# A spectral layer on one core: two images half a block apart, one image's transforms between the pieces of the other's MLP

## What is computed

```python
for i in range(L):                       # 4 blocks
    residual = x
    xn = layer_norm(transpose(x))        # over the 64 channels
    xf = rfft2(xn, norm='ortho')         # 128 x 65, complex
    o1 = relu(xf @ w1 + b1)              # complex, 64 -> 64
    o2 = o1 @ w2 + b2                    # complex
    o2 = o2 * ((|o2r| > 0.01) | (|o2i| > 0.01))
    x = residual + irfft2(o2)
    h = gelu(layer_norm(x) @ mw1 + mb1)  # 64 -> 256
    x = x + (h @ mw2 + mb2)              # 256 -> 64
```

## Time and profile before

| | us |
|---|---|
| median of 3 runs | 4481.55 |
| the profiled execution's own time | 4472.71 |
| its span | 4470.9 |
| TensorE busy | 3373.0 (75%) |
| VectorE busy | 2843.4 (64%) |
| ScalarE busy | 2372.6 (53%) |
| GpSimd busy | 1225.0 (27%) |
| ScalarE table loads in the spectral layer | 28 of 1.28 us |

### The profile page before, as it was taken

The page is one execution under the profiler, slowest core; times in us unless marked ns, Lnnn a source line. Parts: engine busy times, 40 slices in busy tenths (PEclk is TensorE's granted clock), DMA queues, the critical chain, the costliest instruction groups (busy, mean ns, idle before and its releaser), DMA issues. The chain is left out here.

```text
span 4470.9 us, 55410 instructions
## 1 busy us (share of the span) xinstructions
PE 3373.0 (75%) x18880; PEld 2122.3 (47%) x18880; DVE 2843.4 (64%) x4911; ACT 2372.6 (53%) x3931; POOL 1225.0 (27%) x869
## 2 busy tenths in 40 slices
PE   4957777787587878788687878785777778777559
PEld 1744444544263636363535353633545454534327
DVE  3866666666566666664766666656666666638748
ACT  2944545454445454545454545454454545446538
POOL 3321414141214141411131323222141414114232
PEclk9978888898798989898898989897888889889869
DMA  9810000000000000010000000001000000044498
GB/s 253 264 61 1 5 1 5 1 4 38 39 4 1 4 1 4 1 42 39 4 1 5 1 5 1 5 38 42 1 5 1 5 1 4 38 173 143 131 257 248
DMA packets 218637, 209.36 MB, mean 47 GB/s; under 512 B 53344, under 2 KB 181472, under 8 KB 209648
## 3 DMA queue, kind: packets, MB, share of 16 engines
q1 hardware_dynamic: 190832, 174.84, 12.3%
q10 hardware_dynamic: 19552, 16.79, 1.6%
q0 software_dynamic: 7968, 13.99, 1.2%
HBM read 125.84 MB, written 79.69 MB: 46 GB/s over the span
## 5 line engine op out<-in xcount | busy, mean ns | idle before, releaser
L1495 ACT ACTIVATE a_hidden<-a_wide,a_up_b 128x1024 f32<-128x1024 f32 x512 | 545.8, 1111 | 160.8 <-PE a_wide L1606 160.8
L1606 PE MATMUL a_wide<-a_yc,a_up_fold 64*128 64x512 f32 x2048 | 557.0, 666 | 68.2 <-ACT a_yc L1478 63.7
L1515 PE MATMUL a_bank<-a_dft_w,a_y 128*128 128x128 f32 x2048 | 265.4, 297 | 383.5 <-issue 178.4
L1350 DVE TENSOR_TENSOR a_x<-a_bank,a_x 128x512 f32<-128x512 f32 x256 | 177.1, 692 | 558.7 <-PE a_bank L1625 553.4
L1616 PE MATMUL a_bank<-a_hidden,a_down 128*64 128x512 f32 x2048 | 496.0, 605 | 0.0
L1232 POOL TENSOR_TENSOR a_y<-a_x,a_stat 128x512 f32<-128x512 f32 x256 | 265.9, 1043 | 717.8 <-PE a_bank L1595 393.6
L1515 PEld LDWEIGHTS a_bank<-a_dft_w,a_y 128*128 128x128 f32 x2048 | 261.0, 212 | 391.0 <-issue 389.0
L1606 PEld LDWEIGHTS a_wide<-a_yc,a_up_fold 64*128 64x128 f32 x2048 | 189.0, 199 | 400.0 <-issue 222.4
L1595 PE MATMUL a_bank<-a_ident,a_y 128*128 128x128 f32 x1024 | 167.2, 289 | 251.8 <-POOL a_y L1232 251.8
L1557 PEld LDWEIGHTS a_wide<-a_mix,a_o 128*128 128x128 f32 x2080 | 273.7, 191 | 129.8 <-issue 122.4
L1371 DVE TENSOR_REDUCE a_stat<-a_sq 128x16 f32<-128x1024 f32 x224 | 271.2, 1211 | 98.9 <-ACT a_sq L1472 98.9
(11 more groups left out here) (220 smaller groups left out, 6852.5 us busy)
## 6 DMA issues: line engine op xcount, KB each, us to landing
a_g<-turned SPq DMA_DIRECT2D x20, 1024.0 KB, 7.7
box_x<-in_x SPq DMA_DIRECT2D x64, 256.0 KB, 4.4
turned<-box_o SPq DMA_DIRECT2D x64, 256.0 KB, 3.8
rows<-a_x SPq DMA_DIRECT2D x16, 1024.0 KB, 6.9
box_x<-rows SPq DMA_DIRECT2D x16, 1024.0 KB, 23.4
...
```

The lines of the kernel that those rows point to most:

```text
L1495: A(hidden[:, q % 2, j], wide[j][:], ACT.Gelu, bias=up_b[:, HC + j:HC + j + 1]).then_inc(s_hid, 1)
L1515: mm = M(bank[i % 4][:, c * P:(c + 1) * P], y[:, 4 * i + c, :], dft_w[:], start=True, stop=True)
L1606: mm = M(wide[j][:, half * BANK:(half + 1) * BANK], up_fold[cs, j * P:(j + 1) * P], yc[cs, q % 2], start=True, stop=True)
```

## The change

The spectral layer becomes one block without barriers or loops, in which all 16 runs are written out. Run n is image `n // 8 * 2 + n % 2` and layer `n // 2 % 4`: two images alternate. A period (n, q) holds MLP block q of run n; the transforms of run n + 1, the other image, are cut into 59 parts and put between its pieces by a table, with four slots in each block. Periods go from n = -2 (statistics of the first image) to the end of run 15.

```diff
-STRIP_ORDER = (0, 1, 7, 2, 6, 3, 5, 4)
+U_INVERSE, U_FORWARD, U_SPECTRUM, U_BACKWARD, U_NEXT, U_END = 0, 4, 20, 39, 55, 59
+def parts_before(slot):
+    if slot <= 18:
+        return sum(slot > s for s in (2, 4, 16, 17))
+    if slot <= 22:
+        return U_FORWARD + 4 * (slot - 18)
+    if slot <= 41:
+        return U_SPECTRUM + slot - 22
+    if slot <= 45:
+        return U_BACKWARD + 4 * (slot - 41)
+    return U_NEXT + sum(slot > s for s in (45, 46, 50, 52))
...
-        low_banks = [psum(f"bank{i}") for i in range(4)]
-        wide = [psum(f"wide{i}", 2 * BANK) for i in range(2)]
+        wide = psum("wide", 2 * BANK)
+        turned, result = psum("turned"), psum("result")
+        bank = [psum(f"bank{i}") for i in range(4)]
...
-        y = sb("y", [P, C, P])
+        y = [sb(f"y{i}", [P, C, P]) for i in range(2)]
-        xf = sb("xf", [P, 2, BANK])
-        o1 = sb("o1", [P, 2, BANK])
-        mag = sb("mag", [P, 2, 4, 2, C])
+        stage = sb("stage", [P, 2, SH, C])
+        xf = sb("xf", [P, BANK])
+        o1 = sb("o1", [P, BANK])
+        mag = sb("mag", [P, 4, 2, C])
...
+                def mlp_up(i, j):
+                    pe.wait_ge(s_yc, i + 1)
+                    if i or j:
+                        pe.wait_ge(s_hid, HC * i + j)
...
                 def mlp_down(i):
                     pe.wait_ge(s_hid, HC * (i + 1))
-                    if q >= 1:
-                        pe.wait_ge(s_delta, q)
+                    if i:
+                        pe.wait_ge(s_res, i)
...
+                for n, q in periods():
+                    Q = BLOCKS * n + q
+                    mlp = 0 <= Q < BLOCKS * RUNS
+                    if mlp:
+                        mlp_up(Q, 0)
+                    parts(n, q, 0, inverse, forward, spectrum, backward)
+                    if 0 <= Q - 2 < BLOCKS * RUNS:
+                        turn_back(Q - 2)
+                    if 0 <= Q + 1 < BLOCKS * RUNS:
+                        turn(Q + 1)
+                    parts(n, q, 1, inverse, forward, spectrum, backward)
+                    if mlp:
+                        mlp_up(Q, 1)
+                    parts(n, q, 2, inverse, forward, spectrum, backward)
+                    if 0 <= Q - 1 < BLOCKS * RUNS:
+                        mlp_down(Q - 1)
+                    parts(n, q, 3, inverse, forward, spectrum, backward)
-            clear(nc, sems)
-            nc.all_engine_barrier()
```

More of the change, by code:

```diff
@@ new lines, in afno_layers @@
+        centre = room[:, 6 * L * P:6 * L * P + P]
+        s_const, s_wscaled, s_wfold, s_wready = (sem(n) for n in ("const", "wscaled", "wfold", "wready"))
+        s_w = [sem(f"w{i}") for i in range(L)]
+        s_raw = [sem(f"raw{i}") for i in range(2)]
+        s_spill, s_reload = [sem(f"spill{i}") for i in range(8)], [sem(f"reload{i}") for i in range(8)]
+        s_stage_out = [sem(f"stage_out{i}") for i in range(2)]
+        s_stage = sem("stage")
+        s_step, s_act_step = sem("step"), sem("act_step")
@@ L1055, in copy_spectrum, with periods, parts @@
             return copy(g[0:HALF + 1, 1:KW - 1, 1, cs], im[0:HALF + 1])
+        def periods():
+            for n in range(-2, RUNS + 1):
+                for q in range(BLOCKS if n < RUNS else 2):
+                    yield n, q
+        def parts(n, q, s, inverse, forward, spectrum, backward):
+            for u in parts_in(q, s):
+                if u < U_FORWARD:
+                    if 0 <= n < RUNS:
+                        inverse(n, INVERSES // 2 + u)
+                elif 0 <= n + 1 < RUNS:
+                    if u < U_SPECTRUM:
+                        forward(n + 1, u - U_FORWARD)
+                    elif u < U_BACKWARD:
+                        spectrum(n + 1, u - U_SPECTRUM)
+                    elif u < U_NEXT:
+                        backward(n + 1, u - U_BACKWARD)
+                    else:
+                        inverse(n + 1, u - U_NEXT)
         with nc.Block() as block:
@@ L1161, in _ @@
+            @block.scalar
+            def _(act):
+                A = nc.scalar.activation
+                count = [0]
+                with nc.allow_non_contiguous_dma("small weights"):
+                    act.dma_start(centre, const[CENTRE]).then_inc(s_const, 16)
+                    for l in range(L):
                         loads = []
@@ L1663, in afno_layers @@
+        clear(nc, sems)
         nc.all_engine_barrier()
```

1129 lines of the change are left out of this document (539 added, 590 removed).

## The result

The changed kernel takes 4517.37 us (median of 5 runs, 4510.91 to 4528.12), the kernel before in the same session 4473.92 (5 runs). The ratio is 1.010, 95% interval 1.0077 to 1.0124: 1% slower, where 4275 us, 4.6% faster, had been forecast. The number lies inside the range, the direction is wrong. The profiled execution has a span of 4513.4 us, against 4470.9.

The account below looks back on a forecast made before the run. TensorE was nearest to a bound inside the stages, idle between them. Runs of 210 us gave 490 + 2940 + 200 + 98 + 30 = 3758; with 504 for box layers, span 4262, forecast 4275 us, range 3960 to 4560.

Parts of the forecast that it names:

- TensorE's work per run: All matmuls of one run at full clock, summed from the old kernel's product times: 162.6 us.
- the clock: TensorE's granted clock halves beside long gaps, five a run: taken as 5 us, between ends of 0 and 13.
- blocks 12 to 3: MLP blocks 12 to 15 and 0 to 3, without transforms, mlp_down waiting for the residual: 63.3 us a run.
- blocks 4 to 11: MLP blocks with the transforms between: 117 us of TensorE work and 21 of waits, 138 us a run.
- the reload: Strip 1's reload waits for GpSimd's next_y and lands 2 to 5 us late: 3 us a run.
- the forecast run of 210: One whole run: 63.3 + 138 + 3 + 5 = 209, taken as 210 us.
- the backward gap: Ahead of the backward transform TensorE waits for masks queued in VectorE with block 9's sums and root: 9.5 us.
- The port: VectorE masks and roots meeting GpSimd's next_y and fold: taken as 0, otherwise 10 us a run, 150 in all.
- The sum by that rule, 4425: Rival: GpSimd's port and late strips hold VectorE, 10 us a run more; chance 0.10 with its upper part to equal.
- Rival 3: Clock stays down in MLP-only blocks, 32 us a run more, 4755 us; 0.18 with any mixture above 4504.
- Rivals 1 and 4: TensorE stays the bound, runs 175 to 190, 3900 us, chance 0.20; table loads, some 80 us a run, under 1%.
- Start and end: Forward transform starts about 356, first MLP block about 490; 30 us for staging copies; box layers 504 behind.

Follow-up runs that it names:

- run 2: Not an experiment: one layer of one image, one of 16 runs inside the changed kernel, profiled in windows: 223.8 us, TensorE busy 183.12 and idle 40.7.
- experiment 7: The split kernel with GpSimd's next_y and fold cut to 4 of 64 channels: 4070.58 us; also ten extra products on the kernel of experiment 6: 4270.16 us.
- the split kernel: The changed kernel with the reduction of squares and the root behind the next residual in blocks 9, 12, 13, 0 and 1: 4237.05 us, ratio 0.9475.
- experiment 4: The changed kernel with ten unused products of 128 columns ahead of mlp_down in blocks 1, 2, 13 and 14: 4464.52 us, ratio 0.9983.
- experiment 1: The changed kernel with VectorE's sums and roots behind the next residual: six MLP-only blocks 4462.8 us, block 9 only 4380.25, all blocks 4370.29.
- experiment 3: The changed kernel with GpSimd's next_y and fold cut to 4 of 64 channels, so another output: 4388.82 us, ratio 0.9817.
- experiment 6: The split kernel with half of the 88 weight loads issued by SyncE instead of ScalarE: 4206.81 us, ratio 0.9403.
- run 14: Not an experiment: the last but one of the 16 runs inside the changed kernel, 197.8 us, forecast as 200 with half the sums.

## Why the forecast was wrong

**The step that failed is TensorE's work per run**, the sum of 162.6 us at full clock with 5 for the clock: 167.6. Run 2 of the changed kernel has 183.12, 15.5 more. The waits were forecast as 38.9 (17.9 in blocks 12 to 3, 21 in blocks 4 to 11) and 3 for the reload, 41.9, and measured as 40.7. So of the 14 us that lie between the forecast run of 210 and the measured 223.8, all lie in the busy time, by these windows.

The trace divides the 15.5. In five stretches of run 2 the granted clock is 0.5 (992.3 to 999.2, 1053.8 to 1057.2, 1125.5 to 1139.1, 1180.1 to 1183.5, 1190.3 to 1197.1). The sum of their windows:

```profile
sum 34.10, PE 22.05 PEld 10.33 DVE 17.40 ACT 5.08 POOL 16.31; mean PE 4.41 PEld 2.07 DVE 3.48 ACT 1.02 POOL 3.26
```

TensorE is busy for 22.05 us of these 34.10. At the higher clock that work would take about half (eight products 1.94 us instead of 3.68), so as an estimate the clock costs 11.0 us where 5 stood, and at full clock the work is 172.1 us where 162.6 stood. **Both terms of the sum were too small, the work by 9.5 us and the clock by 6.0.**

Part of that could have been seen. The windows of the forecast give 2851.99 us of busy time in the layer, 178.2 for each of 16 runs, and 175.24 in run 1. Of these 17.03 fall at the lower clock, by the same count, so the old run needs 166.7 us at full clock, and 4.1 us of the 9.5 are missing from the forecast's reading of the old kernel already. The other 5.4 came with the change, and closing the gaps doesn't remove them. The kernel with the fewest gaps, in experiment 7, has this run:

```profile
899.80:1094.30 194.50, 175.44 (x976) 105.87 (x974) 126.86 (x240) 118.12 (x180) 31.67 (x42) 0.98 0.13 44
```

At a clock of 0.98 TensorE is still busy 175.44 us, 172.7 of them at full clock by the same estimate; the split kernel's run has 172.5. The forecast took distances between starts from the old kernel's longer trains. Cut into pieces, the same products stand further apart at full clock. The two halves of an up product take 1.06 us each to the next start (1171.58 to 1172.63 above), where the old one took 1.92 for both (674.71 to 676.63). A piece of the backward transform takes 3.77 (1141.91 to 1145.68) for 16 products, where the forecast has 3.53. A chunk of the spectrum takes 2.75 (1068.29 to 1071.04) for 2.65, an inverse piece up to 1.91 (1167.80 to 1169.71) for 1.72. With 16 blocks, 8 pieces of the transforms, 16 chunks and 8 inverse pieces that makes about 8 of the 9.5 us. Why a cut costs this was not tested.

By groups, the forward transform's products took 14 us less in all (297 ns before, 282 after), and mlp_down took 76 more, the up product 51 and mix 36. Experiment 4, which raises the clock in the four blocks, gives back 73 of the 76, 26 of the 51 and 3 of the 36: in mlp_down it was the clock, in mix hardly at all.

**Blocks 12 to 3.** Forecast 63.3, with 3 and some of the 5 on top; measured 71.9. The long and the short ones are those forecast: blocks 13, 14, 1 and 2 long, blocks 15, 12, 3 and 0 short, though block 13, without its inverse piece, is as long as block 14 and not shorter. Experiment 1 shows the chain to be the cause, and experiment 4 gives 5.0 of the 8.6 us to the clock. The mechanism was right, its consequence for the clock too small: a wait of 3.95 us is followed by 1.45 us more in the product.

**Blocks 4 to 11.** Forecast 138, measured 152.8. TensorE's work, 117, was 127.56 in run 2. Of the waits, the backward gap was taken as 9.5 and is 13.3 on the mean; the mix products' wait was taken as 2 and is 6.2. In run 2 the waits of these blocks are 24.4 against 21, those of blocks 12 to 3 are 16.3 against 17.9 and 3 for the reload, so the total of 41.9 was met in part by luck. The queue of masks, sums and root was named rightly: moving block 9's sums, in experiment 1, gave 137 us. The 3.8 beyond it are close to the 3.2 that one pair of masks loses beside GpSimd.

**The port, taken as 0.** Masks have a mean of 803 ns where L1316 had 600, which is 6 us of VectorE's time a run by experiment 3 (370.6 to 277.7 us in all), and that experiment gives 7.5 us a run, GpSimd's own length included. The prediction had priced this as 10 a run and set it aside, "since only strips 0 and 1 fall among the masks". It did not ask what releases GpSimd: the root does, so its normalise instructions start just when VectorE turns to the masks behind the root, and behind another root its fold meets the masks of block 6. The rule of the Trainium skill (SBUF — State Buffer, "SBUF: two separate sides"), a lock held for a whole instruction, agrees with the 4.30 us beside 2.98. The sum by that rule, 4425, is nearer to 4517 than the forecast, and still 92 short of it.

**The clock.** Rival 3, 0.5 throughout the MLP-only blocks, did not come: the granted clock is 0.90 and 0.86 there. It falls behind most of the single waits and returns, 1.94 us for mlp_down in the blocks between. The forecast's 5 us for the whole run are what experiment 4 finds in four blocks of it. The Trainium skill (TensorE: Matmul & The Clock Gate, "HAM oscillation — how this bites in real kernels") says that idle gaps between bursts bring the array back to half rate each time; the product of 3.68 us behind a wait of 3.50, against 1.94, agrees; the wait of 3.01 us with 1.94 behind it shows that it is not each time.

**Rivals 1 and 4.** TensorE did not stay the bound: it waits 12.7 us a run for the residual, and blocks 14 and 2, right behind a root, take 10.5 and 10.6 us and not 5. Table loads did not come either: the changed kernel has one in this layer.

**Start and end.** The forward transform starts at 373.4 instead of 356, and the first MLP block 151 us behind it instead of 130: 34 us in all from 490. ScalarE's issues were costed at 53, and half of them moved to SyncE gave 30 (experiment 6), so that term stands; each strip of the first image took 13.5 us, forecast 14.5. Where the rest of the 17 and 21 us lies wasn't followed up. Runs 6 and 7 cost 49 more than two ordinary ones, not 30. There VectorE waits 37.5 us for reloads of x; experiment 7 leaves these 49 in place (55 there), so it isn't GpSimd, and whether it is ScalarE's copies or the order of SyncE's queue stays open.

The sum: 34 at the start, 231 in runs 0 to 13 (163 of it in the ordinary ones), 2 less in run 14, 4 more in the last, 16 less in the box layers: 251 us, which is 4513.4 less the forecast span of 4262.

**The chances.** Anything above 4504 us had 0.18, for rival 3 and mixtures, and the measured 4517 falls there. The clock was put at 5 of its 0 to 13 us and the port at 0 of 10, as if each were a matter by itself. They are not independent: a late root makes the wait, the wait lowers the clock, and the root's end starts GpSimd on the port.
